# Sixteen maxima of the next batch's first heads moved two slots ahead, and three slots left without maxima, in an attention and feed-forward kernel

## The reference

```python
x_norm = gamma * rmsnorm(x) + beta
q, k, v = split(x_norm @ W_q.T), split(x_norm @ W_k.T), split(x_norm @ W_v.T)
attn = softmax(scale * einsum('bnqd,bnkd->bnqk', q, k), axis=-1)
x = x + a_alpha * (einsum('bnqk,bnkd->bnqd', attn, v) @ W_o.T)
x = x + f_alpha * (silu(h @ gate_w.T) * (h @ hidden_w.T) @ out_w.T + out_b)
```

## Time and profile before

| | us |
|---|---|
| median of 3 runs | 1150.63 |
| the three runs | 1144.51, 1150.63, 3568.11 |
| the profiled execution | 1146.07 |
| its span, first to last instruction | 1144.3 |

### The profile page before, as it was taken

The page is one execution under the profiler, slowest core; times in us unless marked ns, Lnnn a source line. Parts: engine busy times, 40 slices in busy tenths (PEclk is TensorE's granted clock), DMA queues, the critical chain, the costliest instruction groups (busy, mean ns, idle before and its releaser), DMA issues.

```text
span 1144.3 us, 19157 instructions
## 1 busy us (share of the span) xinstructions
PE 1051.4 (92%) x6775; PEld 729.0 (64%) x6775; DVE 792.9 (69%) x1616; ACT 558.1 (49%) x1244; POOL 302.4 (26%) x371
## 2 busy tenths in 40 slices
PE   6589889989998999999899989988988999899997
PEld 6324247755774675577467647753877888787775
DVE  4576777678668766956776786666645875567775
ACT  4256656457556655655574556455553332232221
POOL 2311023213221321322132123201323344333331
PEclk9789999999999999999999999988998999999998
DMA  7924434053324405230541524070211111002111
GB/s 230 191 58 137 78 94 152 5 107 101 105 33 107 155 20 108 77 128 12 98 147 58 67 81 148 2 144 20 71 47 36 52 54 42 29 29 74 56 51 38
DMA packets 89310, 92.70 MB, mean 81 GB/s; under 512 B 11792, under 2 KB 86552, under 8 KB 88192
## 3 DMA queue, kind: packets, MB, share of 16 engines
q1 hardware_dynamic: 87920, 90.31, 30.1%
q10 hardware_dynamic: 1296, 1.18, 0.5%
HBM read 61.68 MB, written 29.78 MB: 80 GB/s over the span
## 4 chain that ended last, share of the span: by engine, by line
PE 77%; DVE 14%; issue 4%; ACT 2%; POOL 2%; DMA 1%; ACTq 0%; POOLq 0%; SPq 0%; DVEq 0%
PE gen L1087 29%; PE core L1087 13%; PE pvb L1199 11%; PE core L1173 8%; PE core L1187 8%; DVE negmax L845 6%; PE gen L1407 2%; DVE xn L821 1%; PE gen L1158 1%; PE pvb L1399 1%; PE gen L1237 1%; ACT xn L642 1%; POOL stat L537 1%; PE pvb L1207 1%; PE gen L1380 1%
## 5 line engine op out<-in xcount | busy, mean ns | idle before, releaser
L845 DVE TENSOR_REDUCE negmax<-core 128x1 f32<-128x512 f32 x512 | 338.3, 686 | 179.8 <-PE core L1173 178.4
L654 ACT ACTIVATE p<-core 128x512 f32<-128x512 f32 x512 | 278.3, 597 | 170.1 <-PE core L1187 167.3
L1173 PE MATMUL core<-kst,qst 96*128 96x512 bf16 x512 | 195.5, 398 | 37.0 <-DVE negmax L845 28.2
L1087 PE MATMUL gen<-hs,wgh 128*128 128x256 f32 x1536 | 220.1, 293 | 8.9 <-DVE a L899 8.9
L1087 PEld LDWEIGHTS gen<-hs,wgh 128*128 128x128 f32 x1536 | 195.8, 189 | 27.5 <-DVE a L899 13.2
L1087 PE MATMUL core<-wup,hp 128*128 128x512 f32 x768 | 192.7, 400 | 0.5 <-POOL hp L600 0.5
L557 POOL TENSOR_TENSOR a<-a 128x256 fp32r<-128x256 f32 x128 | 94.3, 737 | 321.4 <-ACT a L672 321.4
L1187 PE MATMUL core<-qst,kst 99*128 99x512 bf16 x512 | 160.4, 393 | 0.2
L1087 PEld LDWEIGHTS core<-wup,hp 128*128 128x128 f32 x768 | 141.0, 190 | 29.1 <-issue 0.9
L1173 PEld LDWEIGHTS core<-kst,qst 96*128 96x128 bf16 x512 | 46.4, 98 | 156.6 <-DVE negmax L845 78.2
L1199 PE MATMUL pvb<-p,vst 128*32 128x512 f32 x1024 | 126.9, 614 | 0.0
(11 more groups left out here) (156 smaller groups left out, 1184.7 us busy)
## 6 DMA issues: line engine op xcount, KB each, us to landing
parts_d<-qk SPq DMA_DIRECT2D x32, 384.0 KB, 2.7
v_d<-v SPq DMA_DIRECT2D x8, 1024.0 KB, 5.5
vst<-v_d SPq DMA_DIRECT2D x16, 512.0 KB, 5.1
qst<-parts_d SPq DMA_DIRECT2D x96, 64.0 KB, 2.3
qst<-parts_d SPq DMA_DIRECT2D x48, 128.0 KB, 4.4
kst<-parts_d SPq DMA_DIRECT2D x48, 128.0 KB, 7.5
kst<-parts_d SPq DMA_DIRECT2D x90, 64.0 KB, 2.3
xa<-in_x_dram SPq DMA_DIRECT2D x8, 512.0 KB, 5.4
```

The lines of the kernel that those rows point to most:

```text
L654: act.activation(p32[:, ring(b, m), k * S:(k + 1) * S], stb[k], ACT.Exp, scale=SCALE).then_inc(s["exp_"], 1)
L845: dve.tensor_reduce(negmax[:, n // TT, n % TT:n % TT + 1], smb[n % 2], AX_X, ALU.max, negate=True).then_inc(s["smax"], 1)
L1087: last = pe.matmul(out_, l, r, start=start and i == 0, stop=stop and i == len(passes) - 1, **kw)
L1173: pe.matmul(smb[n % 2], qst[0:KROWS, h, q * P:(q + 1) * P], kst[0:KROWS, h, :], start=True, stop=True).then_inc(s["smax_mm"], 1)
```

## The change

A table `N_MAX` says how many maxima steps each of a batch's 32 maxima slots takes, in place of two in each. For all batches but the first the first 16 slots of the stream (slots 18 to 31 of one pass, 0 and 1 of the next) now hold 3, 3, 3, 2, 3, 2, 2, 2, 3, 2, 2, 2, 3, 0, 0, 0. So slots 18, 19, 20, 22, 26 and 30 take three, and 31, 0 and 1 none. By the end of slot 23 the first 16 maxima are there, and their turn moves from slot 26 to slot 24 (`T_TURN_0`). From slot 2 on there are two a slot again, with the same numbers as before. The third one of a slot stands right behind the second, on PE and on DVE. Batch 0 keeps its order.

```diff
+    N_MAX = [3, 3, 3, 2, 3, 2, 2, 2, 3, 2, 2, 2, 3, 0, 0, 0] + [2] * H
+    T_TURN_0 = T_MAX + 6
...
+        def maxima_at(stream, z):
+
+            return [(b, n) for b, m in stream(z, T_MAX)
+                    for n in (range(2 * m, 2 * m + 2) if b == 0 else range(sum(N_MAX[:m]), sum(N_MAX[:m + 1])))]
+
+        def turned_at(at, z):
+
+            late = [(b, g) for g, t in enumerate(T_TURN) for b in at(z, t) if g > 0 or b == 0]
+            return late + [(b, 0) for b in at(z, T_TURN_0) if b > 0]
...
-                    for g, t in enumerate(T_TURN):
-                        for b in at(z, t):
-                            shift_parts(b, g)
-                    for b, m in stream(z, T_MAX):
-                        maxima(b, 2 * m)
+                    for b, g in turned_at(at, z):
+                        shift_parts(b, g)
+                    for b, n in maxima_at(stream, z)[:1]:
+                        maxima(b, n)
...
-                    for b, m in stream(z, T_MAX):
-                        maxima(b, 2 * m + 1)
+                    for b, n in maxima_at(stream, z)[1:]:
+                        maxima(b, n)
...
-                    turned = [(b, g) for g, t in enumerate(T_TURN) for b in at(z, t)]
+                    turned, largest = turned_at(at, z), maxima_at(stream, z)
                     for b, g in turned:
                         shift_turn(b, g)
                     if not turned:
-                        for b, m in stream(z, T_MAX):
-                            scores_max(b, 2 * m)
+                        for b, n in largest[:1]:
+                            scores_max(b, n)
...
                     for b, g in turned:

                         need(pe, "shift_c", 4 * NG, b, 4 * g + 2)
-                        for b2, m in stream(z, T_MAX):
-                            scores_max(b2, 2 * m)
-                    for b, m in stream(z, T_MAX):
-                        scores_max(b, 2 * m + 1)
+                        for b2, n in largest[:1]:
+                            scores_max(b2, n)
+                    for b, n in largest[1:]:
+                        scores_max(b, n)
```

More of the change, by code:

```diff
@@ L62, in build @@
     T_TURN = [T_MAX + 2 * GROUP * (g + 1) for g in range(H // GROUP)]
+    N_MAX = [3, 3, 3, 2, 3, 2, 2, 2, 3, 2, 2, 2, 3, 0, 0, 0] + [2] * H
+    T_TURN_0 = T_MAX + 6
+    assert len(N_MAX) == STEPS and sum(N_MAX[:6]) == 4 * GROUP and sum(N_MAX) == 2 * STEPS
     T_ST = T_MAX + 11
```

## The result

| | before | changed |
|---|---|---|
| median of 17 runs, us | 1146.35 | 1153.56 |
| lowest run | 1141.58 | 1148.41 |
| ratio, 95% interval | | 1.0066 (1.0051 to 1.0080) |
| span of the profiled execution | 1144.3 | 1153.2 |

The account below looks back on a forecast made before the run. PE bounds the kernel as a whole, DVE slots 31, 0 and 1. Per pass 2.94 - 1.76 = +1.2 us, six times +7.1, plus 3.7 in the first pass: +10.8 on 1146.07, about 1157 us, range 1146 to 1168.

Parts of the forecast that it names:

- What bounds the slots: Slots 31, 0 and 1 are DVE's, PE waiting for reductions; in slots 18 to 30 DVE waits for PE.
- Slots 18, 19, 20 and 22: Third maxima matmul and its wait for the bank cost PE 0.95, 0.51, 0 and 0.22 us a pass.
- Slot 24: Moved turn needs all 16 maxima, and the slot's maxima matmuls wait for DVE's splitting: cost 1.16 us a pass.
- What is given back: Slots 31, 0 and 1: `turn_o` starts 1.76 us earlier a pass, bounds 1.5 and 1.95.
- The first pass: Pass 0: extra reductions and uncovered splitting on DVE cost 3.7 us (bounds 1.5 and 4.5); nothing comes back.
- The load in later passes: Second half's load, needed in slot 2, lands 5.1 us after issue, at most 5.8, ahead of need; no cost.
- Rival 5: The load of the second half becomes late in every pass and swallows the gain: 1168 us; chance 0.05.
- The clock: Seven 1.2 GHz stretches of PE, one a pass behind the waits of slots 31 to 3, remain; 1.4 us each.
- the four signs of being wrong: Slot 24 grows under 0.8 us, slot 18 under 0.6, slot 31 to `turn_o` above 4, low-clock stretches not seven.
- Rival 2: The clock no longer falls as PE's poor stretch shortens; seven times 1.4 us come back: 1147 us; chance 0.15.
- The third maximum hidden (3): Waits in slots 18, 19 and 24 shrink to 0.22, 0.22 and 0.3 us: 1144 us; chance 0.10.
- A fall of the clock in the late slots (4): New waits drop PE to 1.2 GHz among dense products: one more stretch a pass 1167 us, two 1177; chance 0.10.

Follow-up runs that it names:

- the moved matmuls: Changed kernel with the third maxima matmul of slots 18 and 19 issued behind that slot's gate and hidden matmuls; 1148.55 us, ratio to before 1.0026.
- the version without one there: Changed kernel with the third maximum of slot 18 moved to slot 23; one run of 1153.68 us.
- the run meant to test the first pass by itself: Changed kernel with batch 1 as well as batch 0 left in the old order; one run of 1146.44 us.

## Why the prediction was right

It said 1157 us, +10.8 on its base, and within 2%; measured is +7.6 by the ratio, inside the range. The mechanism it named, new waits in the late slots that outweigh the freed ones, is what the slots show. The total is partly luck: a term that was 2.2 us too large and a wait of some 2.2 us that was left out cancel. And where it took 2% for what a measurement can tell, 17 runs of each kernel tell 0.15%.

- **What bounds the slots.** Right. Slots 31 to 1 were DVE's and are now ACT's; the late slots are PE's, and there each wait is paid in full.
- **Slots 18, 19, 20 and 22.** Right within 0.1 us each, and the moved matmuls show that three quarters of slot 18's cost and half of slot 19's is the wait.
- **Slot 24.** Right: the turn waits for the sixteenth reduction and the maxima for the splitting. Slots 23 to 26 grew by 1.16 against 1.26. (Its own terms end the second splitting instruction at 424.68 + 0.59 = 425.27 and not 425.31, a slip of 0.04.)
- **What is given back.** 1.76 us was too little, and 1.94 was at its upper bound of 1.95. The term was sized by ACT's pace in the last pass, 1.17 to 1.2 us a slot; it ran at 1.08. So the net of a pass was +0.8 and not +1.2 us, or +4.9 and not +7.1 in six passes.
- **The first pass.** The direction was right, the size of 3.7 too large. By the slots of pass 0 that ran at the full clock slots 18 to 28 grew by about 2.9 us: slots 19 to 28 by 2.3, and slot 18 by 0.6, taking for its length without a third maximum the 3.78 us of the version without one there, since the kernel before ran slot 18 at the lower clock. Slots 31 to 1 gave back 1.2 us and the wait for the load took 1.34, so nothing came back, as forecast. That is 3.0 us, and with the 4.9 us above 7.9; this sum was made afterwards, and the run meant to test the first pass by itself did not settle it.
- **The load in later passes.** Here a step failed. The prediction let it arrive ahead of need, by a transfer's median of 5.1 us and at most 5.8. Those were the figures of one pass, in which the issues were held up; in the pass before, the view gives 7.9 and at most 9.0, since the transfers are issued 0.47 us apart and land about 1 us apart. So the load arrives up to 1.5 us late, 2.4 us in passes 2 to 7 of one profile and 2.1 in the other. Rival 5 had the right place, but its price is some 0.4 us a pass and not 1.76.
- **The clock.** It was kept at seven stretches, and a number other than seven was one of the four signs of being wrong. That sign came up: the windows of the seven passes hold 8 in one profile of the changed kernel and 5 in the other (and 8 in the kernel before, whose pass 7 has a second one that the forecast did not count). The single price, 1.4 us, was right. Rival 2, that the stretches are saved, is partly borne out in passes 2 to 6, where six of the ten windows above have none, and not in passes 1 and 7. What this is worth over many runs can be estimated from the mean granted clock that each run reports: 0.9665 in the mean of the changed kernel's 17 runs, 0.9646 in 42 others of the kernel before. The difference is 1.3 stretches, or some 2 us at 1.4 to 1.6 each: an estimate, since these figures don't tell where in the program the stretches fall. 7.9 us, 2.2 from the load and -2 from the clock make 8.1, against 7.6 measured (5.8 to 9.2).
- **The rivals.** The third maximum hidden (3): only in slot 20, as forecast. A fall of the clock in the late slots (4): none of passes 1 to 6 shows it.

The Trainium skill ("TensorE: Matmul & The Clock Gate", Part 1) says that activity releases the throttle, and the prediction had weighed whether fewer waits would save a stretch. The windows of passes 2 to 6 agree: with the time ahead of `turn_o`, in which PE waited twice for DVE, shortened from 4.76 to 2.87 us, PE ran six of ten passes without any. Those of passes 1 and 7 do not: they have two each. In pass 1 PE waits 3.05 and 3.51 us for the load, and in pass 7 1.50 and 1.03; that these waits bring the second stretch was not tested.

## What to carry to other kernels

Before moving work from a slot where one engine waits to one where it doesn't, ask what the moved instruction will wait for in its new place, and what stands ahead of that on the other engine: here one matmul cost 0, 0.17, 0.23, 0.5, 0.93 or 1.4 us by place alone. Before shortening a stretch, ask what else has to be ready at its end, and read a load's landing in several passes: one pass said 5.1 us, the one before it 7.9. A third use of two banks within a slot belongs behind the longest piece of independent work, not behind the second. And move only as many as the freed slots pay for: four of six maxima brought the whole gain, since another engine became the bound.

## What the hardware showed that was not expected

The stretches at 1.2 GHz move and double between executions of one program: in the same five passes one profile has four and the next has one, which alone makes some 4 us. The changed kernel's runs also spread further, 1148.4 to 1159.7, than the 1141.6 to 1150.6 of the kernel before (without the one of 3568). A single run is no verdict on 2 us here, while the slot lengths at the full clock repeat to 0.1 us. Six loads of 128 KB, issued 0.47 us apart on one queue, land about 1.0 us apart, so the later ones take longer from issue to landing, 9.0 us for the last.
